# Decoder with two cross-attentions: one clip in four of the first cross-attention moved from VectorE to GpSimd

## The reference, cut to what matters

```python
attn = jnp.einsum('bhqd,bhkd->bhqk', q, k) * scale
attn = jnp.clip(attn, -CLAMP, CLAMP)
attn = jax.nn.softmax(attn, axis=-1)
x = jnp.einsum('bhqk,bhkd->bqhd', attn, v).reshape(B, Nq, Cq)
return x @ Wo + bo
```

## Time and profile before

| what | value |
|---|---|
| median of three runs | 1333.36 us (1332.97 to 1979.34) |
| the profiled execution | 1329.35 us |
| its span, first to last instruction | 1327.6 us |
| TensorE busy, share of the span | 90% |
| VectorE / ScalarE / GpSimd busy | 56% / 42% / 7% |
| mean granted TensorE clock | 0.956 |
| X0, first to last E2 | 215.9 to 482.1 us of the span |

### The profile page before, as it was taken

The page is one execution under the profiler, slowest core; times in us unless marked ns, Lnnn a source line. Parts: engine busy times, 40 slices in busy tenths (PEclk is TensorE's granted clock), DMA queues, the critical chain, the costliest instruction groups (busy, mean ns, idle before and its releaser), DMA issues.

```text
span 1327.6 us, 20645 instructions
## 1 busy us (share of the span) xinstructions
PE 1193.6 (90%) x7754; PEld 754.9 (57%) x7754; DVE 742.4 (56%) x1099; ACT 556.9 (42%) x1070; POOL 89.6 (7%) x127
## 2 busy tenths in 40 slices
PE   5999887899999986889599999999999999998887
PEld 3454444233332234778367777767777777777545
DVE  3346476888898845453256554655455554554322
ACT  1343332555555641221156663655334444453230
POOL 1112211000000003000000000000000000000120
PEclk9898877999999987999799999999999999999989
DMA  5010002000000002000242331223443333120000
GB/s 169 9 49 18 8 1 64 0 1 1 1 1 1 1 1 80 0 0 1 68 119 65 80 80 33 65 64 81 113 120 80 80 81 81 31 50 1 0 16 16
DMA packets 46917, 57.47 MB, mean 43 GB/s; under 512 B 12635, under 2 KB 25446, under 8 KB 46822
## 3 DMA queue, kind: packets, MB, share of 16 engines
q1 hardware_dynamic: 43062, 52.48, 16.3%
q10 hardware_dynamic: 3760, 3.67, 0.9%
HBM read 15.23 MB, written 3.15 MB: 14 GB/s over the span
## 4 chain that ended last, share of the span: by engine, by line
PE 79%; DVE 9%; issue 6%; ACT 3%; POOL 1%; DMA 1%; SPq 1%; POOLq 0%; ACTq 0%; DVEq 0%
PE p_unit L1531 21%; PE p_ring L1531 11%; PE p_ring L1632 9%; PE p_out L1655 8%; PE p_ring L1551 8%; PE p_ring L1598 7%; PE p_out L1621 6%; PE p_unit L1716 2%; PE p_ring L1576 2%; PE p_unit L1675 1%; DVE probT_b L1341 1%; PE p_ring L1590 1%; DVE stats L1244 1%; POOL m_z L1064 1%; PE p_ring L1569 1%
## 5 line engine op out<-in xcount | busy, mean ns | idle before, releaser
L1153 ACT ACTIVATE probT_b<-p_ring 128x512 f32<-128x512 f32 x144 | 84.5, 598 | 260.4 <-PE p_ring L1632 260.0
L1311 DVE TENSOR_REDUCE halves<-p_ring 128x2 f32<-128x1024 f32 x128 | 155.6, 1218 | 40.9 <-PE p_ring L1576 40.7
L1341 DVE COPY probT_b<-p_ring 128x512 f32<-128x512 f32 x112 | 77.4, 691 | 174.0 <-PE p_ring L1632 174.0
L1135 ACT ACTIVATE prob_a<-p_ring 128x1024 f32<-128x1024 f32 x128 | 130.7, 1023 | 93.8 <-PE p_ring L1598 93.8
L1293 DVE TENSOR_REDUCE nmax<-p_ring 128x2 f32<-128x1024 f32 (+1 forms) x128 | 155.9, 1218 | 23.5 <-PE p_ring L1551 23.5
L1121 ACT ACTIVATE prob_b<-p_ring,nmax 128x512 f32<-128x512 f32 (+1 forms) x192 | 158.7, 835 | 2.6 <-DVE nmax L1293 2.3
L1551 PE MATMUL p_ring<-stacks 128*128 128x512 f32 x512 | 150.8, 417 | 4.5 <-ACT prob_b L1121 4.5
L1632 PE MATMUL p_ring<-ident,prob_b 128*128 128x128 f32 x1024 | 134.6, 274 | 0.0
L1632 PEld LDWEIGHTS p_ring<-ident,prob_b 128*128 128x128 f32 x1024 | 115.8, 141 | 27.7 <-issue 25.8
L1598 PE MATMUL p_ring<-x_q,x_kq 32*128 32x512 f32 x512 | 126.5, 656 | 0.0
L1551 PEld LDWEIGHTS p_ring<-stacks 128*128 128x128 f32 x512 | 87.0, 190 | 17.0 <-ACT prob_b L1121 5.1
(11 more groups left out here) (201 smaller groups left out, 1658.6 us busy)
## 6 DMA issues: line engine op xcount, KB each, us to landing
stacks<-splitH_b SPq DMA_DIRECT2D x144, 128.0 KB, 2.4
stacks<-splitL_b SPq DMA_DIRECT2D x144, 128.0 KB, 2.4
a_st<-a_image SPq DMA_DIRECT2D x64, 32.0 KB, 1.8
ctx_raw<-in_ctx ACTq DMA_DIRECT2D x1, 1536.0 KB, 15.5
x<-in_x ACTq DMA_DIRECT2D x2, 512.0 KB, 5.2
k_words<-in_L_ffn_k SPq DMA_DIRECT2D x1, 1024.0 KB, 6.7
a_wq<-in_L_attn_Wq SPq DMA_DIRECT2D x1, 1024.0 KB, 6.2
a_wo<-in_L_attn_Wpost SPq DMA_DIRECT2D x1, 1024.0 KB, 9.3
```

The lines of the kernel that those rows point to most:

```text
L1135: nc.scalar.activation(prob_place(key), slot_of("S2", key), ACT.Exp, accum_out=x0_sums[:, m:m + 1]).then_inc(done["E2"], 1)
L1311: nc.vector.tensor_reduce(to, src, AX.X, ALU.max, negate=True).then_inc(done["M1"], 1)
L1341: keep_turned(dve, key, lambda o, i: nc.vector.tensor_copy(o, i)).then_inc(done["VD"], 1)
```

## The change

Of the 16 clips of a group of X0, the four with odd j and pr = 1 get the kind CP and are issued on GpSimd, with the same operation on the same operand; VectorE keeps the other twelve (kind CL). In all 32 of 128 clips move. PV waits for whichever engine clipped its two items. A PV whose second clip is a CP (odd j) is added when the CP is at least three steps old, the others after two as before. A0 keeps its TM.

```diff
+def clipped_by(it):
+
+    return "TM" if it[0] == "A0" else "CP" if it[3] % 2 == 1 and it[4] == 1 else "CL"
...
         for it in clean:
-            sched.add("CL" if it[0] == "X0" else "TM", *it)
+            sched.add(clipped_by(it), *it)
...
-        if adds and age("CL" if adds[0][0] == "X0" else "TM", *adds[0], 1) >= 2:
+        if adds and age(clipped_by((*adds[0], 1)), *adds[0], 1) >= (3 if clipped_by((*adds[0], 1)) == "CP" else 2):
             c = adds.pop(0)
             sched.add("PV", *c)
...
+                elif kind == "CP":
+                    wait(pool, "E2", *key)
+                    t = prob_place(key)
+                    nc.gpsimd.tensor_scalar(t, t, LOW, HIGH, ALU.max, ALU.min).then_inc(done["CP"], 1)
...
-                        wait(pe, "CL" if L == "X0" else "TM", *key, pr)
+                        wait(pe, clipped_by((*key, pr)), *key, pr)
```

More of the change, by code:

```diff
@@ L693, in decoder @@
             "LN": "x_normalised", "XA": "x_rounded", "XD": "x_rest_ready", "FW": "signs_ready",
-            "FS": "hidden_split", "CL": "probs_clipped", "DN": "outputs_kept", "NF": "nans_counted", "GN": "nans_replaced",
+            "FS": "hidden_split", "CL": "probs_clipped", "CP": "probs_clipped_by_pool", "DN": "outputs_kept", "NF": "nans_counted", "GN": "nans_replaced",
             "ZD": "gates_by_dve", "ZA": "gates_by_act", "ZP": "roots_ready",
```

## The result

The median of the kernel after is 1387.23 us (1380.33 to 1392.46, four runs) against 1335.08: a ratio of 1.0393, interval 1.0354 to 1.0432. That is slower, by 52 us where +34 on 1333.36 was forecast, and inside the range. The profiled execution took 1387.27 us, that of before 1329.35. Before X0 it is 6.3 us longer, at a granted clock of 0.86 against 0.90, and after X0 4.7 longer, in stages which the change doesn't touch; X0 itself, from the start of its first S2 to that of its last E2, took 313.2 us in place of 266.4: +46.8.

The account below looks back on a forecast made before the run. A loop through TensorE and ScalarE, not VectorE, was taken as the bound (3.76 us per two steps). Six groups +27, first +1.5, last +4, end +1.5: +34 on 1329.35, 1363; median 4 above, 1367 us; range 1328 to 1415.

Parts of the forecast that it names:

- the wait for DN: Next group's first PV waits 3.0 us after its S2; 1.9 lost, about 0.8 hidden by VectorE's backlog: +1.1.
- The new order: X0's PVs come in pairs; a four-step cycle takes 6.92 us against 7.53, if VectorE keeps up.
- It isn't hidden from VectorE: GpSimd's clip holds up a VectorE clip for its whole instruction: +1.74, VectorE needs about 8.05 us per cycle.
- Rival (a): GpSimd doesn't hold VectorE up: cycles gain 0.45 each (-11), DN costs +7; 1330 us, chance 0.15.
- The length of the clip: A clip on GpSimd takes 2.8 us, bounds 1.23 and 5.6; its own latency is hidden up to nearly 6.
- Rival (c): Clock falls to 0.50 in stretches as TensorE idles: +15 us for a third of X0, 1382; chance 0.05.
- The last group: Last group of X0, without S1, at ScalarE's pace: PVs wait in part for clips held up by CP, +4.
- The first group and the end of X0: First group, half at the lower clock, +1.5; at the end GN waits for GpSimd's last clip, +1.5.
- the pairs of PVs: Sign in the profile of after: PVs come in pairs, pairs about 8 us apart.
- the first PV 3 us behind its S2: Sign: a group's first PV comes 3 us behind its S2, released by ScalarE's L1151 copy.
- under 37 with the long clips: Sign: a group period under 37 us with long VectorE clips present means VectorE wasn't the bound.
- The long VectorE clips: Sign: of 96 VectorE clips some 25 to 32 last 2 us or more, each begun inside a GpSimd clip.

Follow-up runs that it names:

- Order alone: The kernel after with its PV order kept, but all 128 clips on VectorE; 1376.7 us, ratio 1.0271.
- The probe: The kernel before with work added ahead: GpSimd runs a clip, a multiply and an add while VectorE runs 170 small copies; 1351.42 us, one run.
- Order alone, DN first: The kernel after with all clips on VectorE and DN ahead of its step's exponential in ScalarE's order; 1336.74 us, ratio 1.0028.
- DN first: The kernel after, GpSimd clips included, with DN ahead of its step's exponential in ScalarE's order; 1341.13 us, ratio 1.0049.
- The same pairs with the first pair's clips on GpSimd: The kernel before, but even blocks' PVs wait three steps and GpSimd clips the first pair of heads of odd blocks; 1356.3 us, ratio 1.0166.
- Engine alone: The kernel after with its 32 clips on GpSimd, but every PV waits two steps as before; 1353.8 us, ratio 1.0141.

## Why the prediction was right or wrong

**Direction and size.** Slower was right, and 1387 lies in the range, 20 us above the forecast. But the reasons were not those of the forecast, and that the number fell into the range is luck: a hold-up that isn't there in the assumed size had carried most of its sum, and two terms that it had small (the wait for DN) or left out of the sum (the clock) make up the loss. The prediction's own price even leads to the measured time: 3.62 in place of 2.8 at 2.4 us for each 0.1 adds 20 us to 1367. This is chance, as the hold-up that this price stands for is not there. Its chances also don't quite add up: 0.51 + 0.12 + 0.05 make 0.68 for slower, where it has 0.65.

**The new order: right.** Pairs stand 6.85 us apart (325.26 to 332.11), forecast 6.92, before 7.53. The order alone has 6.82.

**The wait for DN: right in place and size, wrong in what hides it.** The PV waits 2.98 (3.0), TensorE stands still for 1.85 (1.9). The forecast let a backlog of VectorE hide 0.8; as VectorE has no such backlog, the whole wait counts, 1.94 per group.

**"It isn't hidden from VectorE": this step failed.** This was the term of +1.74 us per cycle. The row of a VectorE clip of 2.80 beside a GpSimd instruction of 2.35 was read as a rule for every GpSimd instruction, and it was one of another kind than the clip: BA, an add of two inputs. The probe has both kinds. Its add keeps VectorE out throughout; its tensor_scalar takes about 1.0 us at the start and 1.0 at the end. The Trainium skill (SBUF — State Buffer, "Who interferes with whom") has the lock last for the whole instruction; the probe agrees for the add and not for the tensor_scalar, and the measurement decides. In after a VectorE clip that begins 0.3 behind GpSimd's loses about 0.6 (1.28 for 0.68), not 1.74 per cycle. So VectorE has slack, and the chain that was to be 8.05 us per cycle doesn't exist. In a full group this term was the bulk of +4.5; what the clips cost is 0.53. That remainder shows in the waits of TensorE, first in group 2 of after, then in the group of "Order alone, DN first":

```profile
PE p_unit L1725 <- DVE rwide_a L1471: 1.0, 1, 1.0
PE p_unit L1704 <- DVE wide_max L1327: 0.8, 1, 0.8
...
PE p_unit L1721 <- DVE rwide_a L1467: 1.0, 1, 1.0
PE p_unit L1700 <- DVE wide_max L1323: 0.3, 1, 0.3
```

These are units that wait for small VectorE instructions. The first wait, of 1.0, is there without GpSimd's clips too. The second is 0.5 longer with them: the instruction that turns the maxima wide (128x16) takes 0.70 in place of 0.18, from 336.22 to the end of a GpSimd clip at 336.88. Rival (a), "GpSimd doesn't hold VectorE up", was nearer to the mechanism, but its 1330 took the wait for DN at +7 and no clock.

**The length of the clip: mis-sized.** 3.62 where 2.8 was taken from an instruction with one operation; the bounds of 1.23 and 5.6 hold it. In full groups it is hidden, as forecast. Two operations aren't two passes: 2.79 and 3.63.

**The clock: the largest term, and priced least.** Rival (c) gave it a chance of 0.05 and 15 us, and the sum nothing. In the profiled executions X0 is 46.8 longer. At the full clock the parts come to about 18: 2.45 for the pairs (X0 of order alone with DN first, 268.8 us against 266.4, one group of it at 0.94), 1.85 for the clips (X0 of DN first, 270.7), and 1.94 for each of seven groups, 13.6. The other 29 are the clock. That these falls come with this wait is shown from both sides: with DN first X0's groups 1 to 7 keep 1.00 and 46 us are gone from the median, and the late last PV alone brings both the wait and falls of the clock. But the wait doesn't decide it alone. Groups 2 to 4 have it and keep their clock, and so does the last group of before with one wait of 1.8; and "The same pairs with the first pair's clips on GpSimd" lost clock in six groups without any wait of TensorE over 1.0. Why the clock falls in one group and not in the next stays open.

**The last group.** +4 was forecast for PVs that wait for held-up clips. With the clock kept (DN first) it is +1.7, 23.78 against 22.09; in after it is +11.35, which is mostly the wait for DN ahead of 509.87 and the clock that falls with it; one wait of 1.0 for a GpSimd clip is the smaller part. With two steps for the PVs, not three, the waits for GpSimd would have been the main loss, as "Engine alone" shows.

**The first group and the end of X0: these two terms didn't come.** +1.5 was forecast for each. The first group took 39.00 as before. At the end GN starts 2.5 us after the start of the last exponential, where before it was 3.2: it starts 1.3 us into GpSimd's last clip, at 536.75, and isn't held up.

Of the signs named, the pairs of PVs, the first PV 3 us behind its S2, and "under 37 with the long clips" decide little, and CP at 3.62 lies inside its bounds. The long VectorE clips aren't there (96 clips, mean 0.76), and this is the sign that says that the step of the hold-up is wrong.

## What to carry to other kernels

Before work is moved in an order written by hand, look at what the last item of a group releases: here one PV, one step later, put a ScalarE copy behind an exponential, and taking this back gained 46 of 52 us, while the change of engine cost 0.5 us in a group of 36. Where an item has only two steps between its slower clip and its use, look at the stage with the shortest steps: there the change of engine alone cost 15 us in the last group, the fallen clock included. Price a new stall of TensorE twice, once as time and once as the clock that can fall behind it; the second was the larger here (about 29 us against 13.6 in the profiled executions). And take a case of contention from a row of the same kind of instruction, with the same number of inputs, or measure it.

## What was not expected of the hardware

A GpSimd tensor_scalar on 128x1024 keeps VectorE's copies out only in about its first and last microsecond (3.63 us long with two operations, 2.79 with one), a tensor_tensor in all of its 2.34. The granted clock of TensorE fell from 1.00 to 0.50 at single waits of 1.85 us in a stretch that was otherwise busy, stayed there for about 17 us twice and for 37 us once, and did this in some groups and not in others that do the same work; in the profiled execution of "DN first", with the wait gone, it didn't fall in any of groups 1 to 7. Runs of one kernel scatter with their clock: "Order alone" took 1364.48 us at a mean of 0.932 and 1389.96 at 0.908.
